# Causal attention stage: both heads' scores as 64-row tiles, short and long rows in pairs, projection in pieces, unrolled

## What is computed

```python
latent_kv = x @ w_kv_down
kv = latent_kv @ w_kv_up
k, v = (kv[..., :HD], kv[..., HD:])
...
q = (x @ w_q).reshape(Bx, Tx, N_HEAD, HEAD_SIZE)
att = jnp.einsum('bqhd,bkhd->bhqk', q, k) * HEAD_SIZE ** (-0.5)
att = jnp.where(causal, att, -jnp.inf)
att = jax.nn.softmax(att, axis=-1)
y = jnp.einsum('bhqk,bkhd->bqhd', att, v).reshape(Bx, Tx, HD)
return y @ w_out
```

## Time and profile before

| | |
|---|---|
| median of 3 runs | 2536.64 us (2535.06 to 2537.02) |
| profiled execution | 2536.69 us, its span 2534.9 us |
| mean granted TensorE clock | 0.965 |
| PE busy over the span | 91% |
| DVE busy, ACT busy | 66%, 56% |
| the causal stage | from 1243.5 us to 1970.1 us of the span |

### The profile page before, as it was taken

How to read it: one execution, slowest core, us unless ns; L and a number is a source line. 1 busy time by engine, 2 the same in 40 slices (tenths; PEclk the granted TensorE clock), 3 DMA queues, 4 the chain that set the end, 5 groups by cost and what they waited for, 6 DMA issues and landing times. The chain is left out here.

```text
span 2534.9 us, 45808 instructions
## 1 busy us (share of the span) xinstructions
PE 2306.7 (91%) x17440; PEld 1111.4 (44%) x17440; DVE 1684.1 (66%) x2107; ACT 1410.7 (56%) x2711; POOL 152.2 (6%) x333
## 2 busy tenths in 40 slices
PE   6899999999977699998899999999999979999977
PEld 3233333333244122223466666666666534444444
DVE  7999999999644899994545445455554364444453
ACT  2788888888914488886454444445545222222233
POOL 3000000000005100000100000000000100000000
PEclk7899999999989699999999999999999989999988
DMA  4000000000001200000000000000000000000000
GB/s 135 9 14 13 8 10 14 14 13 2 2 9 45 74 11 18 27 2 4 17 1 4 4 0 3 3 0 3 3 0 0 23 7 19 17 18 19 16 9 26
DMA packets 42625, 38.66 MB, mean 15 GB/s; under 512 B 9509, under 2 KB 34085, under 8 KB 42352
## 3 DMA queue, kind: packets, MB, share of 16 engines
q1 hardware_dynamic: 40324, 34.56, 4.5%
q0 software_dynamic: 1488, 1.04, 0.2%
q10 hardware_dynamic: 668, 1.04, 0.1%
HBM read 29.85 MB, written 7.36 MB: 15 GB/s over the span
## 5 line engine op out<-in xcount | busy, mean ns | idle before, releaser
L849 ACT ACTIVATE a0p<-ps 128x512 f32<-128x512 f32 x1024 | 542.0, 599 | 113.5 <-PE ps L753 99.1
L859 DVE TENSOR_REDUCE a0nm<-ps 128x2 f32<-128x1024 f32 x512 | 587.8, 1215 | 12.1 <-PE ps L733 10.0
L1478 DVE TENSOR_REDUCE canm<-ps 128x1 f32<-128x128 f32 (+7 forms) x256 | 193.0, 757 | 245.5 <-PE ps L1342 243.9
L767 PE MATMUL ps<-a0p,a0vst 128*32 128x256 f32 x4096 | 328.3, 392 | 25.5 <-ACT a0p L849 14.2
L1342 PE MATMUL ps<-a2k,a2q 96*128 96x512 f32 (+3 forms) x768 | 323.6, 523 | 11.2 <-ACT cap L1440 11.2
L849 ACT ACTIVATE a1p<-ps 128x512 f32<-128x512 f32 x512 | 274.9, 596 | 59.1 <-PE ps L753 50.6
L859 DVE TENSOR_REDUCE a1nm<-ps 128x2 f32<-128x1024 f32 x256 | 295.0, 1215 | 15.7 <-PE ps L733 14.9
L753 PE MATMUL ps<-a0qm,a0k 32*128 32x512 bf16 x1024 | 274.2, 387 | 0.0
L1440 ACT ACTIVATE cap<-ps,canm 128x128 f32<-128x128 f32 (+7 forms) x256 | 188.7, 737 | 88.9 <-DVE canm L1478 88.2
L1677 ACT ACTIVATE ex_s<-ps 128x512 f32<-128x512 f32 x128 | 76.4, 597 | 279.0 <-PE ps L1632 279.0
L733 PE MATMUL ps<-a0k,a0q 32*128 32x512 bf16 x1024 | 203.8, 396 | 28.1 <-DVE a0nm L859 21.8
(11 more groups left out here) (317 smaller groups left out, 2778.2 us busy)
## 6 DMA issues: line engine op xcount, KB each, us to landing
a0parts<-a0parts_sb SPq DMA_DIRECT2D x8, 384.0 KB, 3.8
a1parts<-a1parts_sb SPq DMA_DIRECT2D x8, 384.0 KB, 3.7
ex_wg<-in_ex_gate SPq DMA_DIRECT2D x32, 64.0 KB, 1.8
ex_wu<-in_ex_up SPq DMA_DIRECT2D x32, 64.0 KB, 1.9
ex_wd<-in_ex_down SPq DMA_DIRECT2D x32, 64.0 KB, 1.9
mod_w<-in_L_wmod SPq DMA_DIRECT2D x4, 384.0 KB, 5.4
a0q<-a0parts SPq DMA_DIRECT2D x62, 24.0 KB
a1q<-a1parts SPq DMA_DIRECT2D x30, 48.0 KB
```

The lines of the kernel that those rows point to most:

```text
L767: last = pe.matmul(R.ps[32 * j:32 * j + 32, 6, cols], vst[:, g, s, j * HG // 4, :], p[:, s % 2, j, cols], start=(g == 0 and s == 0 and hal ...
L849: act.activation(p[:, s % 2, e, :], R.ps[:, score_bank(n), :], ACT.Exp).then_inc(exp_done, 1)
L859: dve.tensor_reduce(nm[:, u % 2, tb, 2 - 2 * z:4 - 2 * z, hf], R.ps[:, bank:bank + 2, :], X_AXIS, ALU.max, negate=True).then_inc(bank_free, 1)
L1478: dve.tensor_reduce(nm[:, a % 4:a % 4 + 1], src, X_AXIS, ALU.max, negate=True)\
```

## The change

`causal_stage` is written anew, and its operands are laid out differently.

- q and k of both heads of a pair lie in one tile, head hh on partitions 64 hh to 64 hh + 63, double-buffered over the pairs (`hp % 2`), as v and the weights are. A projected piece is moved by one instruction of 128 partitions. There are 12 pieces now (4 q, 4 k, 4 v of 512 columns), all through banks 4 and 5.
- `score` takes both heads at once: two masks, then for each chunk of 512 columns a matmul of head 0 on rows 0 to 63 and one of head 1 on rows 64 to 127. It waits until both heads of the score before have their exponentials.
- A unit `n` is a pair of row blocks of one batch: a short one (tb = j) and a long one (tb = 7 - j), j = 0 to 3. There are 8 pairs in a step and 64 in all.
- The pieces of the next head pair are spread over the 8 pairs of the current one: 2, 1, 2, 1, 2, 1, 2, 1. For j = 0 and 1 they come after the short row's turns, for j = 2 and 3 after the short row's product (and after the spreads).
- Every group that is moved through banks 4 and 5 (piece, turn, spread) has its mover, "d" for DVE or "a" for ACT, by its kind and no longer by turns.
- All 64 pairs are written out; there is no loop. The loads of the weights of pairs 0 and 1 of heads come with the stage's first loads; the two memsets of POOL are gone.

```diff
-    w, q, k = W.qkv, W.q, W.k
-    v = sb("v", [128, B, 8, C])
-    p = sb("p", [128, 2, 2, T])
-    pT = sb("pT", [128, 2, 2, 8, 128])
+    w, late = W.qkv, W.late
+    q, k = sb("q", [128, 2, B, T]), sb("k", [128, 2, B, T])
+    v = sb("v", [128, 2, B, 8, C])
+    p = [sb("p_short", [128, 2, CW]), sb("p_long", [128, 2, T])]
+    pT = [sb("pT_short", [128, 2, 4, 128]), sb("pT_long", [128, 2, 8, 128])]
...
+    def pieces(n, at_end):
+        hp, j = n // PER_STEP, n % PER_STEP
+        if hp + 1 == STEPS or (n % PER_BATCH >= 2) != at_end:
+            return []
+        first = 3 * (j // 2) + 2 * (j % 2)
+        return [(hp + 1, m) for m in range(first, first + (1 if j % 2 else 2))]
...
+    groups = [(("project", 0, m), "da"[m % 2]) for m in range(PIECES)]
+    for n in range(PAIRS):
+        groups += [(("turn", n, 0, hh, 0), "d") for hh in range(2)]
+        groups += [(("project", *x), "da"[i]) for i, x in enumerate(pieces(n, False))]
+        groups += [(("turn", n, 1, 0, g), "ad"[g]) for g in parts_of(n, 1)]
+        groups += [(("turn", n, 1, 1, g), "da"[g]) for g in parts_of(n, 1)]
+        if ends_batch(n):
+            groups += [(("spread", n, th), "da"[th]) for th in range(2)]
+        groups += [(("project", *x), "da"[i]) for i, x in enumerate(pieces(n, True))]
...
+        def score(n, long):
...
+            if scores_of(n, long):
+                pe.wait_ge(exp_done, scores_of(n, long))
...
             for hh in range(2):
+                pe.matmul(R.ps[:, 2 * hh + end, width - 128:width], R.identb[:], late[:], start=True, stop=False,
+                          skip_group_check=True)
+            for c in range(end + 1):
+                cols = min(CW, full - c * CW)
+                for hh in range(2):
+                    rows = slice(PH * hh, PH * hh + PH)
+                    last = pe.matmul(R.ps[:, 2 * hh + c, 0:cols], q[rows, hp % 2, b, tb * 128:(tb + 1) * 128],
+                                     k[rows, hp % 2, b, c * CW:c * CW + cols], start=c != end, stop=True,
+                                     skip_group_check=True)
+                    if c == end:
+                        last.then_inc(s_full, 1)
...
+        for m in range(PIECES):
+            project(0, m)
+        score(0, 0)
+        for n in range(PAIRS):
+            score(n, 1)
+            if n:
+                product(n - 1, 1)
+            for hh in range(2):
+                turn(n, 0, hh, 0)
+            for x in pieces(n, False):
+                project(*x)
+            for part in parts_of(n, 1):
+                turn(n, 1, 0, part)
+            if n + 1 < PAIRS:
+                score(n + 1, 0)
+            for part in parts_of(n, 1):
+                turn(n, 1, 1, part)
+            product(n, 0)
+            if ends_batch(n):
+                spread(n, 0)
+                spread(n, 1)
+            for x in pieces(n, True):
+                project(*x)
+        product(PAIRS - 1, 1)
...
     def on_dve(dve):
...
+        for n in range(PAIRS):
+            maximum(n, 1)
+            for hh in range(2):
+                move(("turn", n, 0, hh, 0))
+            if n and ends_batch(n - 1):
+                divide(n - 1)
+            for x in pieces(n, False):
+                move(("project", *x))
+            for part in parts_of(n, 1):
+                move(("turn", n, 1, 0, part))
+            if n + 1 < PAIRS:
+                maximum(n + 1, 0)
+            if ends_batch(n):
+                invert(n)
+            for part in parts_of(n, 1):
+                move(("turn", n, 1, 1, part))
...
-            W.qkv = W.tile("qkv", [C, 3, C])
-            W.loads += [(W.qkv[:, i, :], dram[f"L2_w{n}"][:, 0:C]) for i, n in enumerate(("q", "k", "v"))]
-
-            W.q, W.k = W.tile("q", [96, 2, B, T]), W.tile("k", [96, 2, B, T])
-            W.zeroed = nc.alloc_semaphore("a2zeroed")
+            W.qkv = W.tile("qkv", [C, 2, 3, C])
+            W.loads += [(W.qkv[:, hp, i, :], dram[f"L2_w{n}"][:, hp * C:(hp + 1) * C])
+                        for hp in range(2) for i, n in enumerate(("q", "k", "v"))]
...
-                pool.memset(W.q[PH:96], 0.0).then_inc(W.zeroed, 1)
-                pool.memset(W.k[PH:96], 0.0).then_inc(W.zeroed, 1)
```

More of the change, by code:

```diff
@@ L1242, in causal_stage @@
     STEPS = HEADS // 2
[L1243 to L1256, removed]
-            for hh in range(2):
[L1258 to L1350, removed]
-            if not first:
-                pe.wait_ge(t_d if g % 2 else t_a, hp * (NG // 2) + g // 2)
-            if kind == "turn":
-                hh, part = x
-                pe.wait_ge(exp_done, hp * (2 * I) + (2 * i + hh + 1))
-                for s in range(4 * part, min(4 * part + 4, items[i][1] + 1)):
-                    last = pe.transpose(R.ps[:, 4 + g % 2, (s % 4) * 128:(s % 4 + 1) * 128],
-                                        p[:, i % 2, hh, s * 128:(s + 1) * 128], R.ident[:])
-            else:
-                pe.wait_ge(inv_done, hp * 2 + (i + 1))
-                for n in range(8):
-                    j, hh = n // 2, n % 2
-                    last = pe.matmul(R.ps[PH * hh:PH * hh + PH, 4 + g % 2, j * 128:(j + 1) * 128],
-                                     rinv[:, i, 4 * x + j, hh:hh + 1].broadcast_to([128, PH]), R.ident[:],
-                                     start=True, stop=True)
-            last.then_inc(t_full, 1)
-        def product(hp, i):
-            b, tb = items[i]
-            n = turned_of(i)
-            pe.wait_ge(t_a, hp * (NG // 2) + (n + 1) // 2)
-            pe.wait_ge(t_d, hp * (NG // 2) + n // 2)
-            if i == 0:
-                pe.wait_ge(pj_a, hp * PJ + PJ)
-                pe.wait_ge(pj_d, hp * PJ + PJ)
-            if i % 8 == 0 and not (isinstance(hp, int) and hp == 0 and i == 0):
-                pe.wait_ge(y_done, hp * 4 + 2 * b)
@@ new lines, in causal_stage, with bank_of, scores_of, last_part @@
+    number = {what: g for g, (what, _m) in enumerate(groups)}
+    moved_by_a, moved_by_d = [0], [0]
+    for _what, mover in groups:
+        moved_by_a.append(moved_by_a[-1] + (mover == "a"))
+        moved_by_d.append(moved_by_d[-1] + (mover == "d"))
+    def bank_of(what):
+        return 4 + number[what] % 2
+    def scores_of(n, long):
+        return 2 * (2 * n + long)
+    def last_part(n, long):
+        return number["turn", n, long, 1, parts_of(n, long)[-1]]
+    def on_sp(sp):
+        for hp in range(2, STEPS):
+            sp.wait_ge(t_full, number["project", hp - 2, PIECES - 1] + 1)
+            for i, n in enumerate(("q", "k", "v")):
+                sp.dma_start(w[:, hp % 2, i, :], dram[f"L2_w{n}"][:, hp * C:(hp + 1) * C]).then_inc(w_loaded[hp % 2], 16)
@@ new lines, in on_pe, with projected, turned @@
+        product(PAIRS - 1, 1)
+    def projected(hp, m):
+        if m < 8:
+            b, t = chunk(m % 4)
+            return (q if m < 4 else k)[:, hp % 2, b, t], PH ** -0.5 if m < 4 else 1.0
+        b, t = chunk(m - 8)
+        s = t.start // 128
+        return v[:, hp % 2, b, s:s + 4, :].rearrange("p s c -> p (s c)"), 1.0
+    def turned(n, long, hh, part):
+        blocks = min(4, row_tile(n, long) + 1 - 4 * part)
+        return pT[long][:, hh, 4 * part:4 * part + blocks, :].rearrange("p s t -> p (s t)"), blocks * 128
```

261 lines of the change are left out of this document (158 added, 103 removed).

## The result

| | before | after |
|---|---|---|
| median | 2536.83 us (2535.06 to 2538.57, 4 runs) | 2479.82 us (2477.74 to 2480.42, 4 runs) |
| ratio after / before, 95% interval | | 0.9774 [0.9757, 0.9791] |
| profiled execution: time, span | 2536.69, 2534.9 us | 2479.46, 2477.7 us |
| causal stage, first projection to last division | 726.7 us | 668.8 us |
| one step at the full clock | 89.8 us | 82.65 us |

The account below looks back on a forecast made before the run. PE, busy 91% of the span, was taken as the bound. Stage after: 13.5 + 16 x 40.9 - 12.2 + 2.9 = 658.3 us against 719.7, gain 61.4, so 2536.7 - 61.4 = 2475.3 us; range 2440 to 2532.

Parts of the forecast that it names:

- Part 1: Causal stage scores: float32 matmuls of two heads on 64-row tiles run fully at once, saving 123 us of PE.
- Part 2: PE mode changes in the causal stage: 7 a pair instead of 4, 1.25 against 0.60 us, +42 us of PE.
- Part 3: Order of PE, DVE and ACT work in the pairs, written out: 40.9 us a batch, 4.7 of PE idle.
- Part 4: Ends of the causal stage: prologue 13.5 us, 6.1 less in each last-step batch, last product 1.5, division 1.4.
- The clock: PE's clock in the causal stage: 7 us lost to the 1.2 GHz level before, the same loss kept after.
- Rival C: PE's clock drops after an idle hole in each of 16 batches, 2 to 4 us each: 2500 to 2532; chance 0.08.
- The sum: Causal stage at the full clock from 719.7 to 658.3 us, gain 61.4, whole kernel 2475.3.
- Edits at nothing: Extra weight loads at the stage's head, POOL's memsets, later loads and loop removal cost nothing; uncovered loads would cost 2 to 3 us.
- Rival A: Float32 score tiles don't run at once, so 123 us come back: 2598 us, slower; chance 0.13.
- Rival B: In the scores, the second head runs one record behind the first: 2519 us; chance 0.09.
- Rival D: DVE's chain leaves PE no idle time in the batches: 75 us less, 2400, half of it 2438; chance 0.05.

Follow-up runs that it names:

- the second experiment: The changed kernel with its scores contracted over all 128 partitions instead of two 64-row tiles, so both heads are summed: 2544.52 us, ratio 1.0035 to the kernel before.

## Why the prediction was right, point by point

**Part 1, the scores.** Predicted 123 us of PE, 15.4 a step; measured 30.72 us of score streams a step before and 15.61 after, 15.1 less. The shape bf16 row tiles had shown and the type float32 column tiles had shown carried over together.

**Part 2, mode changes.** Predicted +42 us; measured (4.76 + 5.22) - (2.89 + 3.75) = 3.3 a step, 27 in all. The price was right: 9.98 / 50 = 0.20 each, holes of 0.092 to 0.098. The count was too high. The prediction had 56 a step after and 32 before; a change behind an idle stretch left no hole of its own (in after, from 1272 on, PE starts 0.054 to 0.056 us after the end of what it waited for in all 48 waits with a change of mode, and in 72 of 78 without, 0.146 in the rest), and the trace has 50 and 30 that do. The weight loads of scores and pieces are longer in before, as the prediction has it: 0.195 and 0.19 us on average, a turn's 0.142, a product's 0.136.

**Part 3, the order.** The timetable written out by hand held within 0.25 us for each pair:

| pair | predicted | measured (both batches of a step) |
|---|---|---|
| 0 | 10.33 | 10.53, 10.47 |
| 1 | 9.90 | 10.10, 10.13 |
| 2 | 10.36 | 10.45, 10.52 |
| 3 | 10.29 | 10.21, 10.24 |
| batch | 40.9 | 41.3 |

It had 9.4 us of PE idle a step; 9.94 were measured. (The terms of a pair that it adds to 9.05 are 9.09, so by its own table the idle time is 9.0.) What it said of the cause was right only in part. It named DVE's order, two maxima in a row ahead of the moves. The run with one-block maxima took 14.1 us of DVE's work out of a step, and 6.6 of the 9.9 us of waits stayed, all of those before turns among them; a third was the maxima's. The run with the moves ahead of the maxima was slower. The run with four banks gave 4.8 us a step (82.65 to 77.81). By the trace of after, 3.6 us of the waits are turns that wait for a move, 3.4 are pieces in the middle that wait for one, 1.9 are masks that wait for the short row's exponential, and 1.1 are pieces at the end. A timetable with right lengths gives the right sum, but doesn't tell which of the things that are late together would have to go: that the sum came out so well is no proof of the cause it named.

**Part 4, the ends.** Prologue 13.5 predicted, 14.4 measured (twelve pieces 11.4 instead of 10.7; ACT's table load, at 1259.26, took 1.28; first mask of a long row at 1261.41). Without pieces the last step's first seven pairs took 61.1, where with them they take 72.4. Last step with the tail: 72.5 predicted, 72.8 measured.

**The clock.** 7 us were kept as lost. The trace gives the granted clock as a share of full speed, and the two levels that the prediction names in GHz are 1.00 and 0.50 there. It was 0.50 from 1261.5 to 1264.9 and from 1268.3 to 1271.8; PE had stood idle 2.27 us before 1261.41 and again before 1267.90. The first step took 85.65, the six after it 82.65 each: 3.0 lost. In before three of the first seven steps were longer than 89.79, by 6.9 in all. So the clock gave back 4 us that nobody had forecast. That is luck, and no part of the mechanism: at the full clock the stage gained 54 us, not the 61.4 of the sum. Rival C had the clock falling in each of 16 batches; from 1271.8 to the end of the stage it did not fall (1.00).

**The sum.** Predicted stage 658.3 at the full clock, measured 668.8. The 10.5 between are 0.9 prologue, 7 x 0.89 = 6.2 in the steps (82.65 for twice 40.88), 3.0 clock and 0.3 last step and tail. The predicted stage with the 7 us kept for the clock was 665.3, so the gain was 57.9 where 61.4 was expected. The profiled executions differ by 57.2, so 0.7 was lost outside the stage. The 4.5 us between 2475.3 and 2479.8 are thus some 7.5 us of work and waits that the sum lacked, less 4 from the clock, and 1 outside the stage and in rounding.

**Edits at nothing.** The loads: SP's weight loads of this stage were issued until 1232.93, the last of them

```profile
1232.49 0.44 SPq L300 DMA_DIRECT2D a2qkv<-in_L_wv  x1
```

and PE's first matmul with them starts at 1247.01, 14 us later, released by PE's own sequencer and by no transfer:

```profile
1247.01 3.86 PE L1319 MATMUL ps<-h_res,a2qkv 128*128 128x512 f32 x8 [0.94 <-PEq L53]
```

The prediction set them against 1238.75, the first matmul that reads `a2down`; `a2qkv` is first read at 1243.47 in before, so the cover was larger than it said. The loop was nothing, by its own run. The 1.1 us that the prediction calls the loop's entry stand at the head of the stage, ahead of the step that was written out already, and after has 0.94 there.

**Rival A** was wrong, and its price too: 2598 took back the whole 123. The run without concurrency gave 2544.5. What failed in it is "123 us back": the added 15.1 us of stream a step displace 4.1 of waits. They displace 3.0 of mode changes as well, but only because that run has no row tiles; two row tiles that don't overlap would keep them. For these an estimate from the table is 2544.5 + 8 x 3.0 = 2568, slower than before by 1.2% instead of 2.4%; no run had them. If the loss is even in between, the kernel is no faster once 57 / 88 = 0.65 of the concurrency is gone, not half.

**Rival B**, in which the second head of a score runs one record behind the first (2519 us, the author's estimate), is settled by the eight records in 1.99 us, in after and in the run with the heads written one after the other: four slots and not five. Records of one tile follow each other by 0.429 us in the second experiment, so by that estimate a fifth slot would have taken it to some 2.4.

**Rival D** was priced at 75 us for all of PE's idle time; four banks and a better placed piece brought 49 of it. So its price was real, but its condition was not DVE's chain alone.

## What to carry to other kernels

When a contraction has 64 rows or fewer, look whether two of them can lie on rows 0 to 63 and 64 to 127: here that halved 39.6 us of scores a step, and it alone made the gain (without it the rest was 0.35% slower than before). Then count how long a bank of PSUM is gone from its first matmul to the end of its move, and divide by the banks that take turns: giving two dead banks to the turns brought 37 us, nearly two thirds of what the whole change did, while moving instructions past each other on DVE only swapped one wait for another. Before costing a slow-down at its full busy time, ask which waits it fills.

## What the runs showed of the hardware

- Float32 matmuls on two 64-row tiles ran side by side in full: the scores of a step took 19.8 us where they had taken 39.6.
- They ran pairwise in both orders in which they were written: 2479.9 us head by head, 2479.8 interleaved. The second of two started 13 or 14 ns after the first in long scores written head by head, 6 or 7 otherwise; what pairs them is not shown.
- A change between tile shapes on PE (64\*128, 128\*64, 128\*128) left a hole of 0.092 to 0.098 us in the three kernels whose steps were added up, and none that could be seen when PE had been idle: it started 0.054 to 0.056 us after the end of what it waited for, in all 48 waits of after with a change and in 72 of 78 without.
- Writing out all 8 steps of the kernel before cost nothing: 0.9995 [0.9986, 1.0005].
- Two idle stretches of PE of 2.27 us near the head of the stage were each followed by a stretch of 3.4 us at 0.50 of the full clock; the later steps, with idle stretches of up to 1.12 us, had none.
